# One core, eight stacked blocks: the fp8 product and the eight-head attention written as one pipeline by batch

## What is computed

```python
def fake_quant_fp8(t):
    amax = jnp.max(jnp.abs(t))
    scale = 448.0 / jnp.maximum(amax, 1e-12)
    return (t * scale).astype(jnp.float8_e4m3fn).astype(jnp.float32) / scale
...
# sixth: one scale for the whole of layernorm(x)
x = x + tanh(g_ffn[2]) * (einsum('bsd,od->bso', fake_quant_fp8(layernorm(x)), fake_quant_fp8(weight)) + bias)
# seventh: 8 heads of 64, over the context of the same batch
q, k, v = layernorm(x) @ Wq, ctx @ Wk, ctx @ Wv
attn = softmax(einsum('bihd,bjhd->bhij', q, k) * 64 ** -0.5)
x = x + tanh(g_xattn[3]) * (einsum('bhij,bjhd->bihd', attn, v).reshape(B, Nq, 512) @ Wo + bo)
```

## Time and profile before

| | us |
|---|---|
| median of 3 runs (1618.54 to 1620.81) | 1619.43 |
| profiled execution, its own time | 1622.06 |
| its span | 1620.3 |
| busy: PE, DVE, ACT, POOL | 1211.6, 1017.7, 688.1, 548.5 |

### The profile page before, as it was taken

One profiled execution on the slowest core, in us unless ns is written; L12 is line 12 of the kernel. 1 busy time (PEld: TensorE's weight loads), 2 busy tenths in 40 slices (PEclk: granted clock), 3 DMA queues, 4 the chain that ended last, 5 costly groups with the idle time before them and its releaser, 6 DMA issues. The chain is left out here.

```text
span 1620.3 us, 31081 instructions
## 1 busy us (share of the span) xinstructions
PE 1211.6 (75%) x10597; PEld 822.1 (51%) x10597; DVE 1017.7 (63%) x3901; ACT 688.1 (42%) x1990; POOL 548.5 (34%) x758
## 2 busy tenths in 40 slices
PE   2277664666677678965989882578888879999997
PEld 2154222343344446643777771255556556777765
DVE  6346759999991498633677776664645554534442
ACT  2133335665664344311445441164646453433342
POOL 5978876887864365313232310000000000000000
PEclk9569875757667799975999996689999898898988
DMA  6400040000003211000000000000000000000001
GB/s 150 126 2 2 1 116 8 20 24 17 28 20 108 71 37 34 14 14 7 2 3 3 3 3 0 11 1 10 0 10 10 1 1 1 1 0 0 0 0 52
DMA packets 64560, 36.94 MB, mean 23 GB/s; under 512 B 24053, under 2 KB 61553, under 8 KB 64435
## 3 DMA queue, kind: packets, MB, share of 16 engines
q1 hardware_dynamic: 63130, 35.02, 7.9%
q10 hardware_dynamic: 1304, 0.33, 0.1%
HBM read 25.21 MB, written 6.42 MB: 20 GB/s over the span
## 5 line engine op out<-in xcount | busy, mean ns | idle before, releaser
L2693 DVE SCALAR_TENSOR_TENSOR k_X<-ps,m_gt,k_X 128x128 f32 (+1 forms) x256 | 72.1, 344 | 126.0 <-PE ps L2592 126.0
L2622 ACT ACTIVATE m_hid<-ps,k_b 128x512 f32<-128x512 f32 x128 | 81.8, 684 | 138.1 <-PE ps L2592 127.7
L2592 PEld LDWEIGHTS ps<-k_w,m_hid 128*128 128x128 f32 x1024 | 123.1, 192 | 26.8 <-issue 17.2
L2583 PE MATMUL ps<-m_xnT,k_w 128*128 128x512 f32 x256 | 131.1, 644 | 1.1 <-DVE m_lg L2638 1.1
L2592 PE MATMUL ps<-k_w,m_hid 128*128 128x128 f32 x1024 | 123.4, 275 | 0.0
L2476 ACT ACTIVATE l_p<-ps,l_shift 128x128 f32<-128x128 f32 x256 | 89.9, 377 | 73.9 <-DVE l_shift L2521 73.9
L2114 DVE TENSOR_REDUCE g_top<-ps 128x8 f32<-128x1024 f32 x64 | 75.4, 1219 | 50.7 <-PE ps L1982 50.7
L121 POOL TENSOR_TENSOR m_rstd<-m_ve,k_half 128x8 f32<-128x8 f32 x4 | 6.5, 1636 | 286.3 <-DVE m_ve L114 286.3
L1379 DVE MATCH_REPLACE8 c_left<-c_top,c_left 128x128 f32<-128x128 f32 x384 | 100.9, 275 | 0.0
L2062 ACT ACTIVATE g_pT<-ps 128x1024 f32<-128x1024 f32 x64 | 62.1, 1022 | 84.9 <-PE ps L1998 84.9
L121 POOL TENSOR_TENSOR l_rstd<-l_ve,k_half 128x8 f32<-128x8 f32 x4 | 6.5, 1636 | 234.6 <-DVE l_ve L114 234.6
(11 more groups left out here) (523 smaller groups left out, 3275.7 us busy)
## 6 DMA issues: line engine op xcount, KB each, us to landing
v_toep<-kpad SPq DMA_DIRECT2D x4, 1024.0 KB, 10.6
fo_dram<-c_fo SPq DMA_DIRECT2D x32, 128.0 KB, 1.7
v_late<-kpad SPq DMA_DIRECT2D x4, 1024.0 KB, 10.5
d_fo<-fo_dram SPq DMA_DIRECT2D x8, 512.0 KB, 3.6
k_X<-in_x SPq DMA_DIRECT2D x8, 256.0 KB, 3.6
out<-k_X SPq DMA_DIRECT2D x4, 512.0 KB, 5.3
f_cx<-in_ctx SPq DMA_DIRECT2D x4, 384.0 KB, 4.9
c_cx<-in_ctx SPq DMA_DIRECT2D x4, 384.0 KB, 3.5
```

Source lines behind the costliest of these rows:

```text
L2583: pe.matmul(ps[:, 4 * u + q, :], k.w1_3[:, e, 128 * q:128 * q + 128], xnT[:, u], start=True, stop=True).then_inc(s["hid_ps"].sem, 1)
L2592: m = pe.matmul(ps[:, 4 * u + 2 + e % 2, j * S:j * S + S], hid[:, u, q, j * S:j * S + S], k.w2_3[:, e, q, :], start=q == 0, stop=q == 1)
L2622: act.activation(hid[:, u, q, :], ps[:, 4 * u + q, :], ACT.Gelu, bias=k.b1_3[:, 2 * e + q:2 * e + q + 1]).then_inc(s["hid"].sem, 1)
L2693: dve.scalar_tensor_tensor(out=xj[u][j], in0=ps[:, 4 * u + 2 + e % 2, j * S:j * S + S], scalar=gt[:, u, j, e:e + 1], in1=xj[u][j], op0=ALU ...
```

## The change

One block takes the place of two. Each engine's stream is written out for n from -15 to 33, and in iteration n each does a step for another batch; a group's own steps are hung on it by due(n, lead), which gives group g in the iteration 4g - lead, and on item(n), which gives one of a group's four 128-column slices of keys and queries.

- TensorE, iteration n: scores of batch n+1 (banks 0 to 3); one key slice (bank 6); output product of batch n-1 (bank 7); transposes of batch n (banks 4 and 5, each half behind its own shares); values of batch n+1 (bank 7); one query slice (bank 6); weighted sum of batch n (bank 4); then, by group, the transposes of the normed x (bank 6), of the quantised x (bank 6) or the fp8 product (bank 7).
- ACT: key copy; four exponentials of batch n+1; two copies of the transposed shares of batch n; four exponentials; query copy; by group the copies of xnT and xqT and the fp8 scaling (before on DVE).
- DVE: maxima and shift of n+1; by group the fp8 product's add to X; add of batch n-1; by group exponent and magic; copy of v of n+1; by group the two roundings, or bn_stats and bn_aggr, or the normed rows; reciprocal of n+1; copy oT of n (before on ACT); shares of n+1 in two halves.
- GpSimd: both bias adds (before on DVE, 128x512), and the reciprocal root by group of four.
- Three buffers for p and its sums, two for pT and oT; keys and values read k.cT in place, so the copies to ct go. All waits are on constants.

```diff
...
@@ -2176,7 +2176,7 @@
         fp8_scales(nc, w, ps, k)
-        fp8_product(nc, w, ps, k)
+        fp8_attention8(nc, w, ps, k)
...
-def fp8_product(nc, w, ps, k):
...
-def stage_attention8(nc, w, ps, k):
...
+def fp8_attention8(nc, w, ps, k):
...
+        FIRST, LAST = -15, B + 2
...
+        def due(n, lead):
+            g = (n + lead) // G
+            return g if (n + lead) % G == 0 and 0 <= g < GROUPS else None
...
+        def begun(n, lead):
+            return min(max((n + lead) // G + 1, 0), GROUPS)
...
+        def item(n):
+            g, b = (n + 5) // G, (n + 5) % G
+            return (g, b) if 0 <= g < GROUPS else (None, b)
...
         @block.tensor
         def _(pe):
+            for n in range(FIRST, LAST):
+                if 0 <= n + 1 < B:
+                    i = n + 1
+                    u, cols = batch(i)
+                    pe.wait_ge(q_done, 4 * (i // G + 1))
+                    if i >= 2:
+                        pe.wait_ge(p_done, H * (i - 1))
                     for b in range(4):
+                        for a in range(2):
+                            r = slice(DH * a, DH * a + DH)
+                            m = pe.matmul(ps[:, 2 * (i % 2) + a, 128 * b:128 * b + 128], qT[r, u, b, cols], kT[r, u, b, cols],
+                                          start=True, stop=True)
+                    m.then_inc(sc_ps, 1)
+                g, b = item(n)
+                if g is not None:
+                    pe.wait_ge(q_done, 4 * g + b)
+                    pe.wait_ge(xnT_done, begun(n - 1, 6))
+                    pe.wait_ge(xqT_done, begun(n - 1, 12))
+                    pe.matmul(ps[:, 6, :], k.wk3[:, 128 * b:128 * b + 128], k.cT[:, W * g:W * g + W], start=True,
+                              stop=True).then_inc(k_ps, 1)
+                if 0 <= n - 1 < B:
+                    i = n - 1
+                    pe.wait_ge(oT_done, i + 1)
+                    pe.wait_ge(v_done, min(i + 2, B))
+                    pe.wait_ge(x8_done, begun(n - 1, 11))
+                    for b in range(4):
+                        m = pe.matmul(ps[:, 7, 0:128], oT[:, i % 2, b, :], k.wo3[:, b, :], start=b == 0, stop=b == 3)
+                    m.then_inc(out_ps, 1)
...
+                    for h in range(H):
+                        if h % 4 == 0:
+                            pe.wait_ge(share_done, 2 * n + 1 + h // 4)
+                        m = pe.transpose(ps[:, 4 + h // 4, 128 * (h % 4):128 * (h % 4) + 128], p[:, n % 3, h, :], k.ident[:])
+                        if h % 4 == 3:
+                            m.then_inc(pT_ps, 1)
+                if 0 <= n + 1 < B:
+                    i = n + 1
+                    if n >= 1:
+                        pe.wait_ge(x_done, n)
+                    else:
+                        pe.wait_ge(v_done, i)
+                        pe.wait_ge(x8_done, begun(n - 1, 11))
+                    pe.matmul(ps[:, 7, :], k.cT[:, S * i:S * i + S], k.wv3[:], start=True, stop=True).then_inc(v_ps, 1)
+                g, b = item(n)
+                if g is not None:
+                    pe.wait_ge(k_done, 4 * g + b + 1)
+                    pe.wait_ge(xnT_done, g + 1)
+                    pe.matmul(ps[:, 6, :], k.wq3[:, 128 * b:128 * b + 128], xnT[:, g % 2, :], start=True,
+                              stop=True).then_inc(q_ps, 1)
+                if 0 <= n < B:
+                    pe.wait_ge(pT_done, 2 * (n + 1))
...
+                g = due(n, 6)
+                if g is not None:
+                    pe.wait_ge(xn_done, G * (g + 1))
+                    pe.wait_ge(q_done, max(0, min(n + 6, B)))
+                    pe.wait_ge(xqT_done, begun(n - 1, 12))
...
+                    m.then_inc(xnT_ps, 1)
+                g = due(n, 12)
+                if g is not None:
+                    pe.wait_ge(xq_done, g + 1)
+                    pe.wait_ge(q_done, max(0, min(n + 6, B)))
...
+                    m.then_inc(xqT_ps, 1)
+                g = due(n, 11)
+                if g is not None:
+                    pe.wait_ge(xqT_done, g + 1)
+                    if n + 2 > 0:
+                        pe.wait_ge(v_done, min(n + 2, B))
...
+                    m.then_inc(o8_ps, 1)
         @block.scalar
         def _(act):
+            for n in range(FIRST, LAST):
+                g, b = item(n)
+                if g is not None:
+                    act.wait_ge(k_ps, 4 * g + b + 1)
...
+                    act.activation(kT[:, g % 2, b, :], ps[:, 6, :], ACT.Identity).then_inc(k_done, 1)
+                if 0 <= n + 1 < B:
+                    act.wait_ge(shift_done, n + 2)
...
+                    weights(n + 1, 0)
+                if 0 <= n < B:
+                    for a in range(2):
+                        act.wait_ge(pT_ps, 2 * n + 1 + a)
...
+                        act.activation(pT[:, n % 2, 4 * a:4 * a + 4, :].rearrange("p a b -> p (a b)"), ps[:, 4 + a, :],
+                                       ACT.Identity).then_inc(pT_done, 1)
+                if 0 <= n + 1 < B:
+                    weights(n + 1, 1)
+                g, b = item(n)
+                if g is not None:
+                    act.wait_ge(q_ps, 4 * g + b + 1)
+                    act.activation(qT[:, g % 2, b, :], ps[:, 6, :], ACT.Identity).then_inc(q_done, 1)
...
         def _(dve):
...
+            for n in range(FIRST, LAST):
+                if 0 <= n + 1 < B:
...
+                g = due(n, 10)
+                if g is not None:
+                    dve.wait_ge(o8_ps, g + 1)
+                    dve.wait_ge(xb8_done, g + 1)
+                    dve.scalar_tensor_tensor(out=group(g), in0=ps[:, 7, :].rearrange("p (j d) -> p j d", j=G),
+                                             scalar=k.unscale[:, 0:1], in1=group(g), op0=ALU.mult,
+                                             op1=ALU.add).then_inc(x8_done, 1)
...
-        stages = [stage_front, stage_film, stage_mix, stage_attention16, stage_fp8,
-                  stage_attention8, stage_moe]
+        stages = [stage_front, stage_film, stage_mix, stage_attention16, stage_fp8, stage_moe]
```

More of the change, by code:

```diff
@@ L2341, in stage_attention8 @@
         once = ctx.enter_context(OneTime(nc, "l_"))
-        bo_done = once("bo")
-        block = ctx.enter_context(nc.Block())
-        @block.sync
-        def _(sp):
-            with sp.Fori(0, TURNS) as t:
-                for u in range(2):
-                    s["v_ps"].wait(sp, t, 0)
-                    sp.dma_start(ct[:, u], k.cT[:, bass.ds(t * 2 * W + u * W, W)]).then_inc(s[f"ct{u}"].sem, 16)
+        q8_done, exponent, magic, sum_done, xq_done, xqT_ps, xqT_done, o8_ps, xb8_done, x8_done = (
+            once(n) for n in ("q8_done", "exponent", "magic", "sum_done", "xq_done", "xqT_ps", "xqT_done", "o8_ps",
+                              "xb8_done", "x8_done"))
@@ L2357, in _ @@
         @block.tensor
         def _(pe):
-            def opening(t, part):
-                if part == 0:
-                    s["p"].wait(pe, t, 0)
-                    s["ct0"].wait(pe, t, 16)
-                    for b in range(4):
-                        pe.matmul(ps[:, b, :], k.wk3[:, 128 * b:128 * b + 128], ct[:, 0], start=True,
-                                  stop=True).then_inc(s["k_ps"].sem, 1)
-                else:
-                    s["pT"].wait(pe, t, 0)
-                    for u in range(2):
-                        transpose_tokens(pe, s, t, u, xn, ps[:, 4 + u, :], k.ident[:])
```

385 lines of the change are left out of this document (154 added, 231 removed).

## The result

The changed kernel takes 1578.7 us (median; 1573.9 to 1580.8) against 1620.1 for the kernel before on the same chip: a ratio of 0.974, 95% interval 0.971 to 0.977. Its profiled execution took 1578.42 around a span of 1576.5, 43.6 less than the profiled execution before.

What follows compares the result with a forecast made beforehand. No engine was full, so the order of work was the limit. Terms 36+6.5+161.1+59.9+22+14.4 = 299.9 us against 336.5, 36.6 saved, gave 1583 us; range 1560 to 1605.

Steps and rivals of the forecast that it cites:

- filling: Stage start to first scores, nothing overlapping, key and query products at half clock: 36 us, 28 at full clock.
- last batch: End of the stage: a bare chain from the final scores to the final add, 14.4 us.
- TensorE's iteration: Plain pipeline iteration: scores, key, output, transposes, values, query and weighted sum follow each other in 7.4 us.
- The ring: DVE-ACT-DVE chain once an iteration: maximum, shift, exponentials, copies, reciprocal, oT copy, shares; 7.3 us, as long as TensorE's 7.4.
- rival B: The DVE-ACT-DVE chain takes over from TensorE: +0.6 us an iteration, total 1601 us; chance 0.12.
- signs of being wrong: Late scores 8 us apart, DVE waiting longer for exponentials than TensorE for anything, clock under 0.9 after filling, changed expert stage.
- Wait (a): Bank 6: transposes of quantised or normed x wait for ACT's query copy; the iteration with quantised ones takes 8.2 us.
- The iteration with the fp8 product: One iteration in each group of four: TensorE's 7.4 us plus 0.3 for the product, 7.7 us.
- Wait (b): Bank 7: output product waits 1.8 us for DVE's fp8 add, once a group; that iteration takes 9.7 us.
- GpSimd's lock on the shares: DVE's shares and GpSimd's operations exclude each other: 0.7 us for each of five groups, bounds 0 and 1.9.
- rival C: GpSimd's power and both bias adds all fall on the share path, 3.6 us a group: 1597 us; chance 0.09.
- rival D: Waits let TensorE's clock drop to 1.2 GHz for part of each group, making the kernel slower than before; chance 0.04.

Runs made afterwards that it cites:

- warm filling: Changed kernel plus TensorE products whose results are never read, added before the first scores to raise the clock: 1573.2 us, ratio 0.972.

## Why the prediction was right

The forecast was 1583 and the time 1578.7. Term by term, it forecast a stage of 299.9 and there are 294.3:

```
term                         predicted   measured
filling                         36.0       39.2
first to second scores           6.5        7.4
iterations 0 to 18             161.1      153.7
iterations 19 to 26             59.9       58.5
iterations 27 to 29             22.0       20.9
last batch                      14.4       14.6
```

- **TensorE's iteration, 7.4 by the prediction, is 6.66.** This is the largest mis-sized term. I took each step's start-to-start time from the old iteration, T 1.03 and V 1.06, and they are 0.87 and 0.86 in the new order; O was put at 1.07 and is 0.89, the key product at 1.05 and is 0.97. The same instructions with nearly the same record lengths (1.04 and 1.02 now, 1.09 and 1.13 then) follow each other closer beside other neighbours, and without a wait ahead of them, of which more at the end. The lower bound of that step, four key products at 0.90, was near, but I used it for K and Q alone.
- **The ring, 7.3, is 7.25.** It was summed link by link from the earlier trace rows and met exactly. Because TensorE is leaner than the terms, it is the ring and not TensorE that bounds the late iterations. So the mechanism of rival B, at the size of my own sum and without its 0.6 more, is what happens there; doubling a copy on DVE and a product on TensorE showed it. One of the prediction's signs of being wrong is there too: in the late iterations DVE waits 1.77 us for exponentials and TensorE 1.13 at most. The ring also ate part of TensorE's gain: an iteration without fp8 work (iterations 19 to 26) averages 7.3, not 6.66; one of the eight, 8.71, has a wait for the query copy in it as well.
- **Wait (a), predicted 8.2, is 8.25.** The chain goes from the maximum through the exponentials to the query copy, and hangs on DVE and ACT; so TensorE's shorter steps didn't shorten it, and adding 0.86 us to TensorE left it at 8.25.
- **The iteration with the fp8 product, 7.7, is 6.99**: 6.66 and the 0.33 of the product, predicted as 0.3.
- **Wait (b), 1.8 us for bank 7, is 2.03.** The iteration came out as 9.51 against 9.7. Moving the product to bank 5 shows the cause, and shows what stands behind it: only 1.0 of the 2.03 comes back.
- **GpSimd's lock on the shares, 0.7 a group, is 0.43** (1.71 for the pair in place of 1.28), but not where the sum had it, so the size is near by luck. The prediction had the power and the next group's bias add behind it hold the shares of the iteration with the fp8 add. These shares take 1.28 in every group, with the power (1064.06 to 1065.10) running beside them; the pair that is held is the one before, by the other bias add, of bo. The run without the adds took these 0.42 us away and kept the power. So rival C, in which all three operations fall on the share path, is out. The Trainium skill (SBUF — State Buffer, Who interferes with whom) names such a lock between DVE and GpSimd. By this rule the trace agrees for the shares beside the add of bo, and for the two tensor-scalar operations at 993.01 and 994.25 as well, where the prediction had said that no row shows it and had counted nothing; it doesn't show in the shares beside the power, 128x4.
- **The filling, 36, is 39.2.** 1.9 of the difference is that lock: GpSimd's two adds of the first groups stand beside DVE's first quantise pass, where quantising has no room (1.6 us), and a third beside the first normed rows (at 1003.74, 2.05 us in place of 1.11). The removal of the adds shows it: up to the first key product that kernel takes 12.8 us, where the prediction summed 12.6. The rest is the transposes between the items, 2.4 us with their waits for bank 6 and predicted at 1.6. An item takes 5.52; the prediction's 5.5 is less than twice its own 2.82, which is 5.64, but nearer to the trace. The half clock that I took was there, and is worth 8.4 (predicted 8).
- **The clock.** Two waits of 2.03 us were followed by half clock, 3.4 us together. The prediction saw the place (rival D) but priced it only as what would use up the whole gain, and counted nothing in the forecast. The time lost is a tenth of what D needed.
- **The last batch** is a bare chain, 14.4 by the prediction, which doesn't give its links, and 14.6 by the trace.

Two groups of errors cancelled: short TensorE steps and the smaller lock made the iterations 13.3 us cheaper than the sum (10.8, 1.4 and 1.1 by the table, the first without the falls of the clock), and the filling (3.2), the second scores (0.9), the falls of the clock (3.4) and the last batch (0.2) took 7.7 of it back. The forecast was nearer than its terms, and that is luck. The part that carried it was right: that an iteration costs TensorE's steps or the ring, which are nearly equal, and that a group has one wait for a bank and one for the query copy on top.

What stays open: why only some of the 2 us waits are followed by a fall of the clock. After the same five waits of 2 us it fell twice in the kernel after, three times with the warm filling, and once with oT on ACT; after five waits of 1.6 us (adds left out) once, and after five of 2.5 (one more copy on DVE) once too. It also fell behind the last scores in several of these kernels, with bank 5 for the fp8 product for instance, and not in the kernel after.

## What to carry to other kernels

When a looped stage is unrolled into one pipeline, sum the chain that runs through the in-order queues of the other engines (here maximum, exponentials, copies, reciprocal, shares) link by link beside TensorE's own steps: when they are as near to each other as here (6.66 and 7.25), taking work off TensorE alone gains less than it seems, and each PSUM bank that holds a result until an engine gets round to it is one wait each turn. Such a wait is cheapest to move in the order: give the product a bank whose next use on TensorE comes latest (here 17 us of 294 for the fp8 product and the two kinds of transposes, 3.4 of them falls of the clock that didn't come and 2.6 the filling), and then take the copy off the engine that closes the ring. Price the filling by itself, at the clock that it will have.

## What was unexpected of the hardware

- A step's cost on TensorE depends on what stands around it: eight f32 transposes followed by the values took 0.87 us start to start, but 1.03 followed by the scores; two 512-column products 0.86 in the new order, 1.06 in the old one. Part of it is a wait just ahead. In the kernel after, the values start at 1210.86, right when the add to X (L2491) that they need has ended, at 1210.80, and the query product follows 0.96 us later instead of 0.86; the output product after its 2.03 us of waiting takes 0.96 instead of 0.89. The old values stood behind such a wait each time (0.72 in the earlier trace rows). What the neighbours add beyond that, no run here takes apart.
- After a pause of 2.03 us in a stream that was busy otherwise, the granted clock fell to 1.2 GHz for about 3 us in two cases of five, at 1.7 us each; after a pause of 1.6 us in one of five.
- A DVE tensor-scalar operation of 0.28 us took 1.32, and one of 0.43 took 1.50, beside an add of GpSimd; and it goes the other way too: GpSimd's add, 1.26 us at 1028.74 with DVE idle, took 1.75 at 1065.07 beside DVE's shares and maximum.
